# AdaLN and top-8 router on one Trainium2 core: which piece of x VectorE turns, and where the routing steps stand

## The reference, cut to what matters

```python
# x (64, 128, 2048) f32; condition (64,) picks one of 16 matrices (128, 128) per sample
W = weights[condition]
h = einsum('bct,bcd->bdt', x, W)              # 64 samples: 128 rows of 2048
flat = h.reshape(64 * 128, 2048)
logits = flat @ router_weight.T + router_bias # 64 experts
scores = softmax(logits)
topk_w, topk_idx = top_k(scores, 8)
w_sum = topk_w.sum(-1, keepdims=True)
w_dense = zeros.at[rows, topk_idx].add(topk_w)
out = x + (flat * w_sum + w_dense @ expert_bias)
```

## Time and profile before

| | before |
|---|---|
| median of 3 runs (lowest to highest) | 578.3 us (577.3 to 578.7) |
| the profiled execution, its own time | 578.7 us |
| its span, first to last instruction | 576.9 us |
| busy share of the span: PE, DVE, POOL, ACT | 96%, 81%, 68%, 63% |
| DMA, mean over the span | 265 GB/s, 82% of 16 engines |

### The profile page before, as it was taken

One profiled execution on the slowest core, in us unless ns is written; L12 is line 12 of the kernel. 1 busy time (PEld: TensorE's weight loads), 2 busy tenths in 40 slices (PEclk: granted clock), 3 DMA queues, 4 the chain that ended last, 5 costly groups with the idle time before them and its releaser, 6 DMA issues.

```text
span 576.9 us, 12865 instructions
## 1 busy us (share of the span) xinstructions
PE 555.4 (96%) x3360; PEld 477.3 (83%) x3360; DVE 468.6 (81%) x1054; ACT 362.9 (63%) x772; POOL 392.5 (68%) x456
## 2 busy tenths in 40 slices
PE   5859999999999999999999999999999999999997
PEld 5748888888888888888888888888888888888865
DVE  2558888888888888888888888888888888888874
ACT  3457666767656676666676766667666667676552
POOL 0276677676668667667767766866766776776676
PEclk9879999999999999999999999999999999999999
DMA  8964988788988888998888998888899877889235
GB/s 307 312 148 183 285 270 258 282 266 283 313 257 277 269 272 277 297 268 279 260 284 266 279 314 256 277 264 277 281 295 288 263 266 277 271 270 315 121 147 218
DMA packets 61794, 152.81 MB, mean 265 GB/s; under 512 B 5266, under 2 KB 35986, under 8 KB 53650
## 3 DMA queue, kind: packets, MB, share of 16 engines
q1 hardware_dynamic: 61778, 152.62, 81.6%
HBM read 85.49 MB, written 67.11 MB: 265 GB/s over the span
## 4 chain that ended last, share of the span: by engine, by line
PE 92%; DMA 3%; ACT 1%; DVE 1%; issue 1%; SPq 1%; POOL 0%; POOLq 0%; ACTq 0%; DVEq 0%
PE zt_ps L314 20%; PE xt_ps L302 14%; PE p_ps L362 12%; PE p_ps L367 11%; PE p_ps L364 10%; PE p_ps L363 10%; PE p_ps L368 10%; DMA w_all<-L_cond_weights 3%; PE scores_ps L337 2%; PE scores_ps L346 1%; PE scores_ps L328 1%; DVE e_kept L558 1%; SPq L242 0%; ACT expert_hl L487 0%; ACT x_hi L435 0%
## 5 line engine op out<-in xcount | busy, mean ns | idle before, releaser
L658 POOL TENSOR_TENSOR x_lo<-x_sb,x_hi 128x512 fp32r<-128x512 f32 x256 | 325.7, 1297 | 138.6 <-ACT x_hi L435 137.8
L427 ACT CAST xt_hi<-xt_ps 128x512 fp32r<-128x512 f32 x256 | 149.4, 585 | 142.7 <-PE xt_ps L302 140.7
L513 DVE TENSOR_TENSOR xt_lo<-xt_ps,xt_hi 128x512 fp32r<-128x512 f32 x256 | 173.4, 678 | 77.5 <-ACT xt_hi L427 77.4
L579 DVE SCALAR_TENSOR_TENSOR out_sb<-p_ps,w_sum,x_sb 128x512 f32<-128x512 f32 x256 | 188.5, 736 | 11.7 <-PE p_ps L368 9.9
L435 ACT CAST x_hi<-x_sb 128x1024 fp32r<-128x1024 f32 x128 | 134.1, 1048 | 0.2 <-PE p_ps L368 0.2
L314 PE MATMUL zt_ps<-xt_hi,router_hl 128*128 128x256 f32 x512 | 129.7, 285 | 2.6 <-DVE xt_lo L513 2.5
L314 PE MATMUL zt_ps<-xt_lo,router_hl 128*128 128x256 f32 x512 | 129.2, 285 | 0.0
L302 PE MATMUL xt_ps<-ident,x_sb 128*128 128x128 f32 x784 | 118.9, 277 | 4.3 <-DVE xt_lo L513 4.3
L362 PE MATMUL p_ps<-x_hi,w_hl 128*128 128x512 f32 x256 | 119.6, 467 | 1.9 <-issue 0.5
L314 PEld LDWEIGHTS zt_ps<-xt_hi,router_hl 128*128 128x128 f32 x512 | 98.2, 192 | 8.6 <-DVE xt_lo L513 3.0
L302 PEld LDWEIGHTS xt_ps<-ident,x_sb 128*128 128x128 f32 x784 | 94.7, 144 | 12.7 <-DVE xt_lo L513 4.8
(11 more groups left out here) (40 smaller groups left out, 367.0 us busy)
## 6 DMA issues: line engine op xcount, KB each, us to landing
out<-out_sb SPq DMA_DIRECT2D x126, 512.0 KB, 3.9
x_sb<-x SPq DMA_DIRECT2D x62, 1024.0 KB, 6.6
x_turn<-x SPq DMA_DIRECT2D x120, 128.0 KB, 6.1
x_sb<-x SPq DMA_DIRECT2D x4, 512.0 KB, 6.9
out_sb<-L_ffn_expert_bias SPq DMA_DIRECT2D x2, 512.0 KB, 8.1
out<-out_sb SPq DMA_DIRECT2D x4, 256.0 KB, 2.5
x_sb<-L_ffn_router_weight SPq DMA_DIRECT2D x1, 512.0 KB, 5.2
bias_sb<-L_ffn_router_bias SPq DMA_DIRECT2D x1, 32.0 KB, 14.3
```

Of the source, the lines that this page charges most:

```text
L427: act.copy(xt_hi[:, n % 2, :, r, :], xt_ps[v % 4][:, :].rearrange("p (q c) -> p q c", c=P)).then_inc(xt_hi_ready, 1)
L513: dve.tensor_tensor(xt_lo[:, n % 2, :, r, :], xt_ps[v % 4][:, :].rearrange("p (q c) -> p q c", c=P), xt_hi[:, n % 2, :, r, :].bitcast(F32) ...
L579: dve.scalar_tensor_tensor(out_sb[:, r, cols], p_ps[n % 2][:, :], w_sum[:, o % 2, r:r + 1], x_sb[:, (2 * o + r) % XRING, cols], ALU.mult, ...
L658: pool.tensor_tensor(x_lo[:, r, cols], x_sb[:, (2 * o + r) % XRING, cols], x_hi[:, r, cols].bitcast(F32), ALU.subtract).then_inc(x_lo_read ...
```

## The change

TURNED goes from 3 to 1: the piece that DVE turns is now the second one, so relay stands in slots 0 and 1 (it stood in slots 4 and 5), T is left out in slots 2 and 3, and T stands in slots 6 and 7. The size and number of the `x_turn` loads stay; they read other columns. PE's `score` moves from ahead of P(3) to behind it. On DVE `add_bias` moves behind finish(3), `top` from the end of slot 3 to slot 4 behind xt_low(4), and the wait of `top` for the logits ahead of that xt_low.

```diff
-TURNED = 3
+TURNED = 1
# PE
-                    if mid and v == 3:
-                        score(m, i - 1)
                     if mid and v == 7 and i != 1:
                         turn_kept(m, i - 1)
                     if old:
...
                         project(m, i - 2, v)
+                    if mid and v == 3:
+                        score(m, i - 1)
# DVE
+                    if mid and v == 4:
+                        dve.wait_ge(logits_ready, 4 * m + i)
                     if new:
                         xt_low(m, i, v)
+                    if mid and v == 4:
+                        top(m, i - 1)
...
-                    if mid and v == 3:
-                        if i == 1:
-                            dve.wait_ge(bias_loaded, 16)
-                        add_bias(m, i - 1)
-
-                        dve.wait_ge(logits_ready, 4 * m + i)
...
                         finish(m, i - 2, v)
                     if mid and v == 3:
-                        top(m, i - 1)
+                        if i == 1:
+                            dve.wait_ge(bias_loaded, 16)
+                        add_bias(m, i - 1)
                     if new and (v + 2) // 2 == TURNED and not early(m, i):
                         relay(m, i, v + 2)
```

## The result

The changed kernel takes **562.7 us** (median of 4 runs, 561.9 to 563.5); the kernel before, timed beside it, 578.5. The ratio is 0.973, 95% interval 0.971 to 0.975. The forecast was 563.8 us.

The account below looks back on a forecast made before the run. PE bounds the kernel, waiting 0.47 us per step on late DVE in slot 0; 13.6 us from 29 steps plus 0.9 at the end, start 0, off 578.3 gives 563.8 us; own range 561 to 566.5, whole 560.5 to 570.5.

Parts of the forecast that it names:

- The bound and the wait: PE's list sets the time; 0.47 us per step is waiting on late DVE, all in slot 0, and goes.
- The size per step: Each full step loses its 0.47 us wait, from 17.03 to 16.56 us; 29 x 0.47 = 13.6 us.
- The walk: One step timed from T(0) with PE never waiting, at start-to-start prices; the next T(0) comes at 16.60 us.
- The relays and SC: Slots 0 to 4: relays cost nothing; z_sum ends 0.5 us before SC needs it; unmoved SC would wait 0.6.
- The routing chain: Slots 3 to 0: PE never waits; kept_low ends at 17.23, 0.5 us before L367 at 17.74.
- The start: Program start: between a loss of 0.3 and a gain of 0.6 us, taken as 0, 1 us either way.
- The end: Last pairs: 1.6 us is waiting; between 0 and 1.6 us goes, taken as 0.9.
- DMA: Whole kernel: bytes stay, DMA busy share rises from 0.87 to 0.89, priced at nothing.
- It doesn't do what it says: Rival: relays make DVE late in slots 2 and 3, SC and P4 wait the 0.47; 578 us, chance 0.06.
- Half stays: Rival at L367: SC-to-kept_low chain some 0.75 us longer, half the old wait back; 571 us, chance 0.14.
- `keep` behind POOL: Rival: `keep` starts after POOL's x_low and is blocked; 0.7 us lost per step, 599 us, chance 0.05.

Follow-up runs that it names:

- kernel with neither edit of the start: Against the kernel before: TURNED = 1 and PE's score behind P(3), add_bias and top left in place, e_rest in SBUF, bias copy not earlier; 562.9 us, ratio 0.971.

## Why the prediction was right, step by step

**The bound and the wait.** Right. PE's list sets the time, the wait was the one in slot 0, and it went whole: 1.59 us from T(0) to R(3), as named beforehand.

**The size per step.** Forecast 0.47; measured 0.50 in 28 steps and 0.82 in the last, 14.9 us in place of 13.6. The walk's two reckonings of a step without waiting were 16.56 and 16.60; the measured step is 16.53. Of the 0.07 against the second one, 0.05 is SC, priced like T at 0.44, which takes 0.39 (295.82 to 296.21); the rest lies within the spread of the walk's own prices, and I did not take it apart further. In the last step slot 7 to 0 has no T of a next pair, and there the old wait was longer (1.85 us from P(7) to P(0), now 1.24). I had counted that step like the others.

**The relays and SC.** Right, and shown from both sides: without SC's move 0.88 us a step come back, more than the 0.6 of the walk; an extra 0.59 us of DVE work uses up the cover. The times in the table hold within 0.15 us, but for the end of kept_twice, 0.3 earlier than walked.

**The routing chain.** The walk is right, but its edit is not what made room: `add_bias` and `top` can stay where they were.

**The start.** Forecast 0, measured 0.14 late, and that it came so near is luck. `keep` starts at 32.44, 1.23 us later than before, as worked out (1.2), and is blocked as long. The first L362 comes 2.1 us earlier, at 37.52 against 39.65, more than the 0.9 to 1.8 that I gave for two T less: T(2) and T(3) of that step had also waited, for xt_low behind the blocked `keep`. Timeline of PE in the kernel before:

```profile
35.79 0.66 PE L302 MATMUL xt_ps<-ident,x_sb 128*128 128x128 f32 x4 [2.34 <-DVE xt_lo L513]
38.45 1.12 PE L302 MATMUL xt_ps<-ident,x_sb 128*128 128x128 f32 x4 [2.01 <-DVE xt_lo L513]
```

But kept_low is later than P(0) then, L367 waits for it, and the granted clock is half (0.50, the 1.2 GHz level) from 33 to 44, where it was from 37 to 43: the first step gives back 2.3 us (19.55 against 17.29). Two errors of some 2 us cancelled, and the 1 us that I allowed covers neither alone.

**The end.** Forecast 0.9, measured 0.5. I had taken the middle of 0 and 1.6; the largest part of what stays is TK, which in the second last pair still waits for kept_twice (1.94 us from P(6) to P(7), in both kernels).

**DMA.** Forecast a share of 0.89, measured 0.87 in a step, at 286 GB/s where it was 279; no T waits for a load in the list of waits.

**The rivals.** *It doesn't do what it says* is near to what the turned piece alone does, with SC still ahead of P(3), and that is worse than rated: 588.8 and not 578, since a wait costs more than its lateness. *Half stays* was rated 7 us for 0.24 us of lateness; two kernels that come 0.04 and some 0.2 us too late pay 8 to 12. *`keep` behind POOL* was rated 21 us above the kernel before; with `keep` moved it is 57, since both instructions are blocked. (Of its 74 us above the after kernel, 12 come from the later `keep` by itself, as the kernel with `e_rest` in PSUM shows.) The margin that decides it was forecast at 0.3 us and is 0.39 for `keep`'s first instruction, and 0.25 for its second (284.77 against 285.02): the change stands that near to the worst of its rivals. The kernel before stood nearer, with 0.20 us for the first.

## What to carry to other kernels

When one engine sets the time and another makes it wait at one point of a step, look for the slots in which the second engine idles, and move there work that nobody waits for soon; then walk the step again, since whatever follows the moved work is late next and may need its receiver moved with it, as SC here. Try such moves together: each half can be a loss alone. Leave tenths of a microsecond between a producer and its consumer, and where a VectorE instruction with two inputs in SBUF runs near GpSimd work, put one input into PSUM before tuning the order around it.

## What the runs showed of the hardware

- **A missed hand-over has a step in it.** PE started 0.15 us after the end of a late `z_sum` (turned piece alone, extra instruction) and 0.06 after a late kept_low, and the matmul behind the one that waited started 0.07 to 0.10 us later than it does otherwise. So being 0.04 us late cost 0.27.
- **The block of VectorE by GpSimd is counted by instruction**: 1.10 and 1.29 us for two instructions in a row, against 0.21 and 0.22 alone, and none for the same two with one input in PSUM, though POOL ran the same pieces beside them.
- **The clock near the start.** In the kernel with neither edit of the start and in the one with `e_rest` in PSUM, PE idles some 2.5 us shortly before or at P(0); the first is granted half clock (0.50, the 1.2 GHz level) from 38 to 42 after that, the second 1.00. What PE did before differs only a little (the first goes straight from eight turns into its idle time, the second runs TK in between). Why the one fell and the other did not stays open; it is a part of the 3.7 us.
